# Edge counts for 32 destinations at a time, from split source indices, interleaved with the U and z0 products

## What is computed

```python
xn = layernorm(x)
mean(h) = segment_sum(h[src], dst) / max(deg, 1)
h   = relu(xn @ Ws0 + mean(xn) @ Wn0 + b0)        # GraphSAGE layer 0
gnn = h @ Ws1 + mean(h) @ Wn1 + b1                # GraphSAGE layer 1
q, k = relu(xn @ Wq + bq), relu(xn @ Wk + bk)     # linear attention, 16 heads of 64
mix = (q @ (k.T @ v)) / (L * 64) @ Wo + bo        # per head, v = xn @ Wv + bv
x1  = x + gnn + mix
out = x1 + bitlinear(gelu(bitlinear(layernorm(x1), w1)), w2)   # ternary weights, 8-bit activations
```

## Time and profile before

| | |
|---|---|
| median of 3 runs | 1510.62 us (1509.56 to 1511.81) |
| span of the profiled execution | 1510.1 us |
| PE / DVE / ACT / POOL busy in it | 1467.5 / 745.1 / 477.5 / 15.8 us |
| mean granted clock of TensorE | 0.997 |

### The profile page before, as it was taken

The page is one execution under the profiler, slowest core; times in us unless marked ns, Lnnn a source line. Parts: engine busy times, 40 slices in busy tenths (PEclk is TensorE's granted clock), DMA queues, the critical chain, the costliest instruction groups (busy, mean ns, idle before and its releaser), DMA issues.

```text
span 1510.1 us, 22494 instructions
## 1 busy us (share of the span) xinstructions
PE 1467.5 (97%) x7704; PEld 702.4 (47%) x7705; DVE 745.1 (49%) x1195; ACT 477.5 (32%) x648; POOL 15.8 (1%) x28
## 2 busy tenths in 40 slices
PE   4999999999999999999999999999999999999998
PEld 2454554554444444444444444444444444444444
DVE  6734542423335775553566633226888553333332
ACT  7656663444330122221211212110000053344342
POOL 0000000000000000000000000000000000000000
PEclk9999999999999999999999999999999999999999
DMA  7356663744564000003454411215556130100110
GB/s 306 109 198 242 239 245 103 268 167 154 204 252 156 15 14 28 28 0 105 132 164 132 129 63 42 97 55 195 180 182 184 52 153 29 57 28 28 44 39 29
DMA packets 55514, 183.03 MB, mean 121 GB/s; under 512 B 6177, under 2 KB 14881, under 8 KB 55201
## 3 DMA queue, kind: packets, MB, share of 16 engines
q1 hardware_dynamic: 55456, 182.26, 35.0%
HBM read 158.11 MB, written 24.12 MB: 121 GB/s over the span
## 4 chain that ended last, share of the span: by engine, by line
PE 74%; DVE 14%; DMA 4%; issue 4%; ACT 3%; DVEq 1%; SPq 0%; ACTq 0%
PE ps L1310 35%; PE ps L1637 9%; PE ps L1623 9%; PE ps L1487 7%; PE ps L1414 7%; PE ps L1530 3%; DMA SPLIT<-in_Wneigh 3%; DVE XIN L1116 2%; PE ps L1317 2%; DVE SPLIT L1116 2%; DVE SPLIT L1110 1%; DVE XIN L1110 1%; PE ps L1347 1%; DMA STREAM<-in_w1t 1%; ACT S L455 1%
## 5 line engine op out<-in xcount | busy, mean ns | idle before, releaser
L1310 PE MATMUL ps<-S,XH 128*128 128x512 f16 x2400 | 528.8, 379 | 1.3 <-ACT XH L639 0.8
L1310 PEld LDWEIGHTS ps<-S,XH 128*128 (+1 forms) x2400 | 232.0, 98 | 270.7 <-ACT XH L639 1.0
L1530 PE MATMUL ps<-Zb,AT 128*128 128x512 f16 x800 | 177.3, 382 | 8.6 <-DVE TMP L1132 8.6
L1637 PE MATMUL ps<-S,XH 128*128 128x512 fp8e4 x640 | 143.0, 379 | 1.1 <-ACT XH L705 1.1
L1623 PE MATMUL ps<-S,SPLIT 128*128 128x512 fp8e4 x640 | 141.2, 379 | 0.0
L1530 PEld LDWEIGHTS ps<-Zb,AT 128*128 (+1 forms) x800 | 78.2, 98 | 105.8 <-issue 13.7
L1035 DVE TENSOR_SCALAR STREAM<-HL,srcf 128x1250 f16<-128x1250 f16 x184 | 100.3, 545 | 48.4 <-PE ps L1487 47.9
L1310 PE MATMUL ps<-Zb,XH 128*128 128x512 f16 x480 | 108.8, 387 | 5.2 <-DVE TMP L822 2.9
L1487 PE MATMUL ps<-STREAM 128*128 128x512 f16 x552 | 108.3, 338 | 1.9 <-DVE STREAM L1037 1.9
L1310 PE MATMUL ps<-S,Zb 128*128 128x512 f16 x480 | 103.8, 379 | 0.0
L1414 PE MATMUL ps<-XH,S 128*128 128x512 f16 (+1 forms) x576 | 102.6, 339 | 0.0
(11 more groups left out here) (188 smaller groups left out, 1120.8 us busy)
## 6 DMA issues: line engine op xcount, KB each, us to landing
STREAM<-in_w1t SPq DMA_DIRECT2D x64, 512.0 KB, 4.7
STREAM<-in_w2t SPq DMA_DIRECT2D x64, 512.0 KB, 4.9
STREAM<-in_w_all SPq DMA_DIRECT2D x48, 512.0 KB, 5.8
XIN<-in_x SPq DMA_DIRECT2D x20, 512.0 KB, 5.4
SPLIT<-in_Wneigh SPq DMA_DIRECT2D x16, 512.0 KB, 6.0
SPLIT<-in_Wself SPq DMA_DIRECT2D x16, 512.0 KB, 3.3
u_scratch<-AT SPq DMA_DIRECT2D x10, 512.0 KB, 3.0
XIN<-u_scratch SPq DMA_DIRECT2D x10, 512.0 KB, 5.5
```

Source lines behind the costliest of these rows:

```text
L1310: last = mm(acc[:, n * BANK:(n + 1) * BANK], left(l, kc), right(kc, r)[:, n * BANK:(n + 1) * BANK], start=(kc == 0 and i == 0), stop=(kc = ...
L1530: last = mm(banks(bank + n, 1), ATv[:, s, tile_of(t)], Z[:, r, s, n * BANK:(n + 1) * BANK], start=(s == 0 and r == 0), stop=(s == NT - 1 a ...
L1637: last = mm(banks(4 + h, 1), hid_T[:, j, kc, :], w2q[:, kc, h * BANK:(h + 1) * BANK], start=(kc == 0), stop=(kc == HC - 1))
```

## The change

The counting is done by groups of 32 destinations (GS = 32, NG = 40 groups), and the source index is split in two, tile and place: for an edge, key_m = (source tile) x 32 + (destination mod 32), and key_s = (source mod 128) + 128 x (group). A one-hot of key_m (128x320) and a one-hot of key_s (128x128, which is empty for edges outside the group) then give, in a single matmul of 320 columns, the counts with the sources on the partitions: 32 columns of each of ten blocks of A transposed. Nothing is turned any more. ACT copies them into AT, which is laid out by destination tile. Two buffers (i = 0, 1) hold a quad each, even groups use buffer 0 and odd groups buffer 1. The degrees come from 100 matmuls of AT with a column of ones after the first self product. The groups are counted inside the U products (groups 0 to 19) and inside the z0 products (20 to 39), two per product, ahead of blocks 3 and 6 (both ahead of block 7 in the first). GpSimd adds the biases to x in place, and DVE evacuates U in one step, into HL instead of AT. DVE's stream in tile t is: quads of group 2t, evacuation of tile t - 1, split of chunk t, quads of group 2t + 1.

```diff
+        hots = [stream16[:, 4 * D + i * QUAD * (GW + P):4 * D + (i + 1) * QUAD * (GW + P)] for i in range(2)]
...
+            link(V.tensor_scalar(k_int[0], src, 2, -GS, ALU.logical_shift_right, ALU.bitwise_and))
+            link(V.tensor_scalar(k_int[1], dst, GS - 1, None, ALU.bitwise_and))
+            link(V.tensor_tensor(key_m[:, :], k_int[0], k_int[1], ALU.add))
+            link(V.tensor_scalar(k_int[0], src, P - 1, None, ALU.bitwise_and))
+            link(V.tensor_scalar(k_int[1], dst, 2, -P, ALU.logical_shift_left, ALU.bitwise_and))
+            link(V.tensor_tensor(key_s[:, :], k_int[0], k_int[1], ALU.add))
...
+            def u_pool(t, j):
+                pool.wait_ge(S(f"x_in{j}"), 80 + 8 * (t - j) + 16)
+                nc.gpsimd.tensor_tensor(XIN[:, j, :], XIN[:, j, :], b_out, ALU.add).then_inc(S("xb"), 1)
...
+            def counts_act(tile, j):
+                for i in range(2):
+                    q = 2 * j + i
+                    act.wait_ge(S("a_ps"), tile * 4 + (q + 1))
+                    alone(act)
+                    A(AT[:, bass.ds(tile * NP_, NP_)].rearrange("p (s n) -> p s n", s=NT)[:, :, q * GS:(q + 1) * GS],
+                      ps[:, (2 + 4 * i + j) * BANK:(2 + 4 * i + j) * BANK + GW].rearrange("p (s n) -> p s n", s=NT),
+                      ACT.Copy).then_inc(S("at"), 1)
...
+            def count_dve(g, i):
+                first = dve.value_load(bnd[0:1, 0, bass.ds(g, 1)], min_val=0, max_val=EC - 1)
+                end = dve.value_load(bnd[0:1, 1, bass.ds(g, 1)], min_val=1, max_val=EC)
+                with dve.Fori(first, end, QUAD) as c_:
+                    n = dve.snap(made[i])
+                    dve.wait_ge(S(f"free{i}"), n + 1)
+                    alone(dve)
+                    for j in range(QUAD):
+                        V.tensor_scalar(hot_m[i][:, j, :], iota_m[:, :], key_m[:, bass.ds(c_ + j, 1)], None, ALU.is_equal)
+                        one = V.tensor_scalar(hot_s[i][:, j, :], iota_s[:, :], col("base")[:, bass.ds(g, 1)],
+                                              key_s[:, bass.ds(c_ + j, 1)], ALU.add, ALU.is_equal)
+                    one.then_inc(S(f"hot{i}"), 1)
+                    dve.reg_add(made[i], made[i], 1)
...
+            def u_dve(pair, j, split_too=True, u=True, first=False):
+                t = pair * 2 + j
+                count_dve(t * 2, 0)
+                if u:
+                    u_out_dve(t - 1, 1 - j, first)
                 if split_too:
                     split_chunk(weight(S0), t, j, 24 + t, at("s", WN0))
+                count_dve(t * 2 + 1, 1)
...
+            dve.wait_ge(S("stream_used"), 96)
...
+            def z0_dve(pair, j, split_too=True, z=True):
+                t = pair * 2 + j
+                count_dve(t * 2 + NG // 2, 0)
                 if z:
+                    z_dve("z0", t - 1, 4 * (1 - j), Z0_SCALE)
+                else:
+                    u_out_dve(9, 1)
                 if split_too:
                     split_chunk(weight(S1), t, j, 32 + t, at("s", WS0))
+                count_dve(t * 2 + (NG // 2 + 1), 1)
...
+            def count_pe(g, i, j):
+                first = pe.value_load(bnd[0:1, 0, bass.ds(g, 1)], min_val=0, max_val=EC - 1)
+                end = pe.value_load(bnd[0:1, 1, bass.ds(g, 1)], min_val=1, max_val=EC)
+                at_ = (2 + 4 * i + j) * BANK
+                wait(pe, "at", g - 3)
+                mm(ps[:, at_:at_ + 2], zero[:, :], iota_m[:, 0:2], start=True, stop=False, skip_group_check=True)
+                with pe.Fori(first, end, QUAD):
+                    n = pe.snap(done[i])
+                    pe.wait_ge(S(f"hot{i}"), n + 1)
+                    for q in range(QUAD):
+                        one = mm(ps[:, at_:at_ + GW], hot_s[i][:, q, :], hot_m[i][:, q, :], start=False, stop=False,
+                                 skip_group_check=True)
+                    one.then_inc(S(f"free{i}"), 1)
+                    pe.reg_add(done[i], done[i], 1)
+                mm(ps[:, at_:at_ + 2], zero[:, :], iota_m[:, 0:2], start=False, stop=True, skip_group_check=True)\
+                    .then_inc(S("a_ps"), 1)
...
+                if ready is None:
+                    between = {3: lambda: count_pe(t * 2, 0, j), 6: lambda: count_pe(t * 2 + 1, 1, j)}
+                else:
+                    def between_first():
+                        pe.wait_ge(S("m_lo"), 8)
+                        count_pe(0, 0, 0)
+                        count_pe(1, 1, 0)
...
+            def deg_pe():
+                for t in range(NT):
+                    for s in range(NT):
+                        last = mm(ps[:, DEG_AT + 2 * t:DEG_AT + 2 * t + 2], AT_tile(t, s), one16[:, :],
+                                  start=(t == 0 and s == 0), stop=(s == NT - 1), skip_group_check=True)
+                last.then_inc(S("deg_ps"), 1)
```

More of the change, by code:

```diff
@@ L32 @@
 QUAD = 4
+GS = 32
+NG = NP_ // GS
+GW = NT * GS
 ECP = EC + 2 * QUAD
@@ L206, in steps, with pairs @@
                     body(pair * 2 + (a + j), j)
+        def pairs(eng, a, b, body):
+            with eng.Fori(a // 2, b // 2) as pair:
+                for j in range(2):
+                    body(pair, j)
+        stream_base = [(24 + 8) * 16, (24 + 8) * 16, 24 * 16, 24 * 16]
         block = ctx.enter_context(nc.Block())
@@ new lines, in _ @@
+            made = [dve.alloc_register(f"made{i}") for i in range(2)]
+            for r in made:
+                dve.reg_mov(r, 0)
+            def count_dve(g, i):
[11 more added lines that the diff above has]
+                    dve.reg_add(made[i], made[i], 1)
@@ L1373, in _ @@
             xT_pe(0, 0)
-            pe.wait_ge(S("ones"), 1)
+            pe.wait_ge(S("fills"), 2)
             pe.wait_ge(S("sq"), 1)
@@ L1455, in _ @@
             pe.wait_ge(S("pad0"), 1)
-            def u_pe(t, j, ready=None):
-                wait(pe, "u_t", t - 1)
-                product(banks(4 * j), lambda l, p: qT[:, l, p, tile_of(t)], of(M_s), ready, "m")\
+            done = [pe.alloc_register(f"done{i}") for i in range(2)]
+            for i, r in enumerate(done):
+                pe.reg_mov(r, 0)
+                pe.sem_inc(S(f"free{i}"), 1)
+            def count_pe(g, i, j):
[14 more added lines that the diff above has]
+                    .then_inc(S("a_ps"), 1)
@@ new lines, in u_pe @@
+            def u_pe(pair, j, ready=None):
+                t = pair * 2 + j
+                if ready is None:
[5 more added lines that the diff above has]
+                        count_pe(1, 1, 0)
+                    between = {7: between_first}
+                wait(pe, "u", t - 1)
+                product(banks(4 * j), lambda l, p: qT[:, l, p, tile_of(t)], of(M_s), ready, "m", between)\
@@ L1460, in u_pe @@
                     .then_inc(S("u_ps"), 1)
+            pe.wait_ge(S("iotas"), 4)
+            pe.wait_ge(S("bounds"), 2)
             u_pe(0, 0, ready=0)
-            u_pe(1, 1)
-            steps(pe, 2, NT, u_pe)
-            done = pe.alloc_register("done")
-            pe.reg_mov(done, 0)
-            parts = [(a, min(a + BANK, N)) for a in range(0, N, BANK)]
-            def aT_pe(t):
-                pe.wait_ge(S("a_row"), t + 1)
-                wait(pe, "aT_lo", t)
-                turn(3, lambda k: a_row[:, k * P:(k + 1) * P]).then_inc(S("aT_ps"), 1)
@@ L1476, in aT_rest_pe @@
-            def aT_rest_pe(t):
-                pe.wait_ge(S("aT_hi"), t + 1)
-                turn(3, lambda k: a_row[:, (8 + k) * P:(9 + k) * P], NT - 8).then_inc(S("aT_ps"), 1)
-            def hots(start=False):
-                n = pe.snap(done)
-                for j in range(QUAD):
-                    pe.wait_ge(S("hot_src"), n + (j + 1))
-                    pe.wait_ge(S("hot_dst"), n + (j + 1))
-                    for a, z in parts:
-                        one = mm(ps[:, a:z], hot_dst[:, j, :], hot_src[:, j, a:z], start=(start and j == 0), stop=False,
-                                 skip_group_check=True)
-                    one.then_inc(S("hot_free"), 1)
-                pe.reg_add(done, done, QUAD)
+            u_pe(0, 1)
@@ L1492, in mean_total @@
+            pairs(pe, 2, NT, u_pe)
             def mean_total():
```

248 lines of the change are left out of this document (112 added, 136 removed).

## The result

The changed kernel takes 1574.47 us (median of 4 runs, 1573.76 to 1576.38) where the kernel before takes 1510.2 beside it: ratio 1.0428 [1.0413, 1.0443]. It is 4.3% slower, 18 us above the forecast of 1556 and inside the range of 1528 to 1590, but 2 us above the 1542 to 1572 that the forecast's own case was given. The span of the profiled execution is 1572.3 us, 62.2 more than before.

The account below looks back on a forecast made before the run. TensorE (PE), busy 97% of the span, was taken as the bound. 1510.1 - 114.9 (PE work removed) + 40.6 (added) + 98.0 (waits) + 1.4 (evacuation) + 20 (clock) = 1555.2, about 1556 us; range 1528 to 1590.

Parts of the forecast that it names:

- The degrees: PE after the first self product: 100 two-column matmuls at 0.056 us each, like a turn, 5.6 us; zero-matmul bound 2.
- Waits behind the load: U tiles: the split's load is issued behind the evacuation, so PE waits 8.4 us once in each of tiles 2 to 5.
- Waits within a group: Quads of one group share one buffer, so PE and DVE take turns: cycle 2.5 us, 1.96 idle, 20 such quads.
- The rival's 2.47: Part of (2): issue of two-pointer compares limits DVE's build to 2.47 us a quad instead of 1.57, 26 us over 29 quads.
- I take 0: GpSimd's in-place bias add on x: meeting DVE's split costs 0 to 1 us a tile; counted as 0.
- up to 8 us: GpSimd and VectorE share a port pair by an exclusive lock; by the skill, up to 8 us on top, not summed.
- The clock: PE behind eight waits over 2.9 us (13.6 us) and some 12 slow quads (6 us): +20 us, between 0 and 45.
- The evacuation's +1.4: First h evacuation, at the end of the first edge sum, comes 1.4 us late because the degrees come later: +1.4 us.
- (1): Rival: the clock stays up, so no 20 us of clock loss: 1536 us; chance 0.16.
- (2): Rival, worse waits: DVE's build bound by issue (26 us), or clock low through tiles 0 to 7 (52): 1575 to 1600; chance 0.16.
- (3): Rival: the split is there when DVE comes to it; 55.7 us of waits and the clock loss go: 1480 us; chance 0.08.
- (4): Rival: the loops run otherwise than counted, one or two quads throughout and DVE ahead: near no change; chance 0.03.

Follow-up runs that it names:

- Experiment 1: Changed kernel with SP issuing the Wneigh0 chunk of tile t + 1 before it waits for the evacuation of tile t: 1524.53 us, ratio 1.0097.
- experiment 3: Changed kernel with GpSimd adding the bias to 2 columns of x instead of 1024: 1568.97 us, ratio 1.0404.
- experiment 6: Changed kernel with PE's long U-stage waits filled by 56 (tiles 6 and 7: 30) throw-away matmuls of 320 columns: 1562.72 us, ratio 1.0363.
- experiments 3 and 2: The second of the two is Experiment 1's kernel with GpSimd adding the bias to 2 columns instead of 1024: 1501.88 us, ratio 0.9936.
- ahead_and_in_turn_early: ahead_and_in_turn with one more small GpSimd addition of zeros, in the q operand's padding, at about 300 us: 1464.45 us, ratio 0.9709.
- in_turn_dve_add: ahead_and_in_turn with the biases added to x by DVE ahead of its evacuation instead of by GpSimd: 1469.17 us, ratio 0.9726.
- ahead_and_in_turn: Changed kernel with Wneigh0 and Wself0 chunks loaded ahead in SP's order and one ring of two quads used in turn whatever the group: 1469.85 us, ratio 0.9742.
- experiment 9: in_turn_dve_add with one more small GpSimd addition of zeros, in the q operand's padding, at about 300 us: 1462.05 us, ratio 0.9693.
- experiment 10: The same kernel as ahead_and_in_turn_early: ahead_and_in_turn with one more small GpSimd addition of zeros at about 300 us: 1464.45 us, ratio 0.9709.

## Why the prediction was right, and where it was off

The direction, the mechanism and the range held; the size was low, in the waits and in the clock alike. Made against the spans, the forecast was +45.1 us and +62.2 came; the 17.1 are taken apart here.

- **PE work.** The count stage took 122.9 us where 120.6 follows from the forecast (0.9 of the difference is its wait, the rest clock). A quad takes 0.56 us (490.20 to the closing zero matmul's 490.76), as assumed, and 240 one-hot matmuls ran, as counted. The degrees were mis-sized. Timeline of PE, kernel after:

```profile
768.25 2.64 PE L1610 MATMUL ps<-one,AT 128*128 128x2 f16 x100
770.75 3.71 PE L1581 MATMUL ps<-Zb,AT 128*128 128x512 f16 x11
```

100 matmuls in 2.50 us, 0.025 each, near the bound of the zero matmul and not the turn: -3.1 us.

- **Waits behind the load.** The chain was right link by link: store to ACT's split 7.4 us (491.37 to 498.76) against 7.0, ACT 1.15, split 1.28, wait 8.4 to 8.8 against 8.4. Experiment 1 shows it to be the cause: SP's order alone is worth 50 us, clock and covered additions included.
- **Waits within a group.** The cycle is 2.84 us (487.36 to 490.20) against 2.5, so the wait is 2.28 on the forecast's measure, 2.14 by its bracket, against 1.96. Two steps were mis-sized. The build: I priced the 128-column compare at 0.17 us to the next start, but with two pointers it takes 0.22; four pairs take 1.75 to the next start, and 0.18 of the difference is theirs. The release: from the end of PE's quad to DVE's first compare 0.40 us pass, where 0.25 was taken. The rival's 2.47 was wrong. On top of it, a cycle costs PE 0.55 more at the lower clock. By tiles, forecast and measured (by brackets): t = 1 14.2 and 13.1; t = 2 to 5 49.2 and 51.5; t = 6 6.7 and 7.1; t = 7 4.7 and 5.1; first count tile 4.7 and 5.4.
- **Tile 0.** 18.5 and 23.4. The step that failed is "I take 0" for GpSimd's addition. It said that an addition meeting the split would cost 0 to 1 us; in fact it meets compares, and one lasts as long as the addition beside it, 2.3 to 2.5 us. With the two in tile 0 it cost 4.4 us here (experiment 3). The Trainium skill (SBUF — State Buffer, SBUF: two separate sides) says that a GpSimd instruction and a VectorE instruction in a two-port mode, or with two SBUF inputs, exclude each other for a whole instruction; 2.42 beside 2.34 us agrees as to the whole instruction (which of the two had the port first, 458.12 and 458.15 don't tell, and no row shows the compare's mode), and the "up to 8 us" beside it held with some 5. All waits: 98.0 and 105.6 by brackets, +7.6; on the forecast's measure, 0.15 more for each of 30, 110.1, +12.1.
- **The clock.** 20 and some 29 us (the growth of both stages, 58.9, less 38.1 forecast for them, with 20 in it for the clock, is 20.8, of which 12.1 is waits, so 8.7 more than 20; the rows give 27 in the U stage and 1.7 in the first count tile). The step mis-sized is the count of places: I took the long waits and some 12 quads, but gaps of 2.14 do it too, with the sparse quads between them (experiment 6, at 449.49; in tile 0 all quads from 393.93 on take 1.25), and 25 quads ran at the lower level. It is inside the 0 to 45 given.
- **Small ones.** The evacuation's +1.4 did not come (its next gap was 1.7 us where before it was 2.84), and the U stage began 1.1 later (376.80 against 375.71). Together: +12.1 +8.7 -3.1 -1.4 +1.1 = 17.4 of 17.1.

**Rivals.** (1) is out by the U stage's granted clock of 0.78. (2) in its first form is out (the build is 1.75, not 2.47). In its second form it is out too: in every tile the clock came back, the 18 product matmuls before the long wait take 4.04 us from tile 2 on, the full clock's time, and 27 us went rather than 52. Its time, 1575 to 1600, begins just above the result, whose clock and waits both came out above the forecast. (3) named its price as 56 us without the clock; experiment 1 gave 50 with the clock, less, because the additions came out from under the wait. With the additions gone on both sides (experiments 3 and 2) the load's place gives 67, 71 by the ratios. Its point was right: the load's place in SP's queue decides most of it. (4) is out: the quads are the 60 counted, and DVE was not ahead.

## What to carry over

When work is moved between stages, follow each engine's and each queue's order through one iteration at the new place: who is waited for there that was long done at the old place. Here the same instructions gave +64 us (after) or -44 (ahead_and_in_turn_early), by the place of one DMA issue in SP's stream, a buffer used in turn, and one small GpSimd instruction. And when a wait is removed, look at what it covered, on engines that share something, before counting the gain.

## What the runs showed of the hardware

- **GpSimd pays several microseconds once** ahead of an operation, with no instruction to show for it: 10.52 us in in_turn_dve_add, 6.92 in its early version, about 8 ahead of the first addition in ahead_and_in_turn (386.04), 8.64 in the kernel before. In all but in_turn_dve_add it stands ahead of the first operation other than a MEMSET behind the PARTITION_ALL_REDUCE at 293 us. A small addition moved it, and gave 5 us by the ratios in experiment 9 (7.1 by the medians) and 5 in experiment 10. The Trainium skill (GPSIMD Engine Reference, Instruction dispatch) says that the first call of a freshly loaded kernel pays a load of some 6 us that no row shows; the 6.92 is near it and the other three are above it, and why the delay came at the program's start in experiment 8 no run shows.
- **A compare of 128 columns with two pointers costs as much as one of 320 with one**: 0.22 us to the next start each, against 0.17 for 128 columns with one pointer and 0.46 for 1250.
- **Two-column matmuls with new weights of 128 columns** follow one another every 0.025 us (100 from 768.25 to 770.75).
- **A lower clock does not need a long wait.** Gaps of 2.14 us with four short matmuls between them go with it (0.72 to 1.25 us for the four). One such gap alone does not do it each time: behind that of 490.20 in after, 18 product matmuls take 4.04 us, the full clock's time. And shorter gaps do it when they come in a row: in tile 0 of in_turn_dve_add_early the clock falls behind gaps of 1.16 and 1.11 us and stays down through gaps of 0.7. Its timeline of PE, and two windows:

```profile
384.79 0.81 PE L1528 MATMUL ps<-STREAM 128*128 x4 [1.16 <-DVE STREAM L1068]
386.71 1.00 PE L1528 MATMUL ps<-STREAM 128*128 x4 [1.11 <-DVE STREAM L1068]
...
386.00:387.00 1.00, 0.29 (x2) 0.19 (x2) 0.89 (x5) 0.06 (x1) 0.00 (x0) 1.00 0.00 0
388.00:389.00 1.00, 0.34 (x2) 0.25 (x3) 0.89 (x5) 0.00 (x0) 0.00 (x0) 0.50 0.00 0
```
